# Attention sums shared anew between transfers, VectorE and GpSimd in a transformer block

## The reference

```python
h = _layernorm(x, axis=-1) * (1 + ca) + sa
x = x + ga * _L0_attn_ref(h, ...)      # 32 query heads, 8 key/value heads, head size 32
h = _layernorm(x, axis=-1) * (1 + cb) + sb
x = x + gb * _L0_ffn_ref(h, ...)       # top-2 of 4 experts, each a rank 16 product
```

```python
attn = jnp.einsum('bqhfd,bkhd->bhfqk', qg, k) * scale
att = jax.nn.softmax(attn, axis=-1)
a = jnp.einsum('bhfqk,bkhd->bqhfd', att, v)
```

## Time and profile before

| | |
|---|---|
| median of three runs | 2799.31 us |
| profiled execution | 2796.36 us |
| its span, first to last instruction | 2794.5 us |
| mean granted TensorE clock | 0.996 |
| TensorE busy (matmul) | 2750.2 us |
| VectorE busy | 2178.0 us |
| GpSimd busy | 1906.9 us |
| ScalarE busy | 1529.6 us |

### The profile page before, as it was taken

One profiled execution on the slowest core, in us unless ns is written; L12 is line 12 of the kernel. 1 busy time (PEld: TensorE's weight loads), 2 busy tenths in 40 slices (PEclk: granted clock), 3 DMA queues, 4 the chain that ended last, 5 costly groups with the idle time before them and its releaser, 6 DMA issues.

```text
span 2794.5 us, 49051 instructions
## 1 busy us (share of the span) xinstructions
PE 2750.2 (98%) x14654; PEld 1696.9 (61%) x14654; DVE 2178.0 (78%) x2809; ACT 1529.6 (55%) x3023; POOL 1906.9 (68%) x710
## 2 busy tenths in 40 slices
PE   7999999999999999999999999999999998999998
PEld 4788888884444444444444444444444447888887
DVE  4433334348999999999999999999999958676667
ACT  3211111116777776767777777767776763455454
POOL 2433333317999999999999999999999986111110
PEclk9999999999999999999999999999999999999999
DMA  7544443434444434344344344443444443323332
GB/s 267 182 144 137 147 137 135 135 114 133 92 88 99 91 87 100 85 87 100 85 92 95 85 98 89 91 98 84 96 93 87 99 132 102 114 96 108 113 100 81
DMA packets 167644, 307.05 MB, mean 110 GB/s; under 512 B 50000, under 2 KB 91408, under 8 KB 159504
## 3 DMA queue, kind: packets, MB, share of 16 engines
q1 hardware_dynamic: 158496, 240.05, 29.5%
q0 software_dynamic: 9072, 66.06, 11.6%
HBM read 159.12 MB, written 79.82 MB: 86 GB/s over the span
## 4 chain that ended last, share of the span: by engine, by line
PE 71%; POOL 3%; DVE 2%; issue 1%; ACT 0%; POOLq 0%; DVEq 0%; ACTq 0%
PE back_ps L1354 20%; PE back_ps L1368 17%; PE s_ps L1328 16%; PE s_ps L1944 12%; POOL p_sum L1129 3%; PE back_ps L1993 2%; PE back_ps L1385 2%; PE back_ps L2012 1%; PE back_ps L1965 1%; DVE mx L1243 0%; PE back_ps L1343 0%; ACT h_t L1725 0%; DVE xn L1799 0%; DVE two_sum L1258 0%; PE back_ps L2019 0%
## 5 line engine op out<-in xcount | busy, mean ns | idle before, releaser
L1223 ACT ACTIVATE p_t<-back_ps 128x512 f32<-128x512 f32 x2048 | 1114.6, 596 | 426.6 <-PE back_ps L1354 388.2
L1243 DVE TENSOR_REDUCE mx<-s_ps 128x1 f32<-128x1024 f32 x1002 | 1172.0, 1208 | 81.9 <-PE s_ps L1328 73.9
L1129 POOL TENSOR_TENSOR p_sum<-p_sum,p_t 128x2048 f32<-128x2048 f32 x254 | 1166.9, 4594 | 22.0 <-ACT p_t L1223 5.7
L1354 PE MATMUL back_ps<-q_st,k_st 98*128 98x512 f32 x2048 | 806.2, 434 | 4.2 <-POOL ones L1098 2.4
L1354 PEld LDWEIGHTS back_ps<-q_st,k_st 98*128 98x128 f32 x2048 | 343.9, 187 | 582.2 <-ACT p_t L1223 483.7
L1328 PE MATMUL s_ps<-k_st,q_st 96*128 96x512 f32 x2004 | 634.3, 397 | 0.7 <-DVE mx L1243 0.4
L1368 PE MATMUL back_ps<-p_t,v_sb 128*32 128x512 f32 x4096 | 546.4, 605 | 0.0
L1328 PEld LDWEIGHTS s_ps<-k_st,q_st 96*128 96x128 f32 x2004 | 379.3, 189 | 77.7 <-DVE mx L1243 8.8
L1258 DVE TENSOR_REDUCE two_sum<-p_t 128x512 f32<-128x1024 f32 x256 | 317.5, 1242 | 8.7 <-DMA p_sum<-two_sum 8.7
L574 POOL TENSOR_TENSOR o_lo<-side,o_hi 128x512 fp32r<-128x512 f32 x80 | 104.3, 1304 | 320.8 <-ACT o_hi L544 320.7
L1129 POOL TENSOR_TENSOR p_sum<-p_t 128x2048 f32<-128x2048 f32 x64 | 313.0, 4891 | 9.3 <-ACT p_t L1223 9.3
(11 more groups left out here) (186 smaller groups left out, 2917.9 us busy)
## 6 DMA issues: line engine op xcount, KB each, us to landing
p_sum<-two_sum POOLq DMA_DIRECT2D x63, 1024.0 KB, 6.9
q_st<-q_hi_d SPq DMA_DIRECT2D x128, 256.0 KB, 4.4
stage<-w_mod SPq DMA_DIRECT2D x48, 512.0 KB, 6.4
q_hi_d<-o_hi SPq DMA_DIRECT2D x64, 256.0 KB, 2.0
q_lo_d<-o_lo SPq DMA_DIRECT2D x64, 256.0 KB, 2.1
q_st<-q_lo_d SPq DMA_DIRECT2D x64, 256.0 KB, 4.1
att_d<-a_sb SPq DMA_DIRECT2D x128, 128.0 KB, 2.3
a_f<-att_d SPq DMA_DIRECT2D x32, 512.0 KB, 4.7
```

The lines of the kernel that those rows point to most:

```text
L1129: nc.gpsimd.tensor_tensor(total, before, p_t[:, kt, :, :], ALU.add).then_inc(sum_done, 1)
L1223: nc.scalar.activation(p_t[:, s, c, :], st_ps[:, c % 2, :], ACT.Exp, scale=SCALE)\
L1243: nc.vector.tensor_reduce(mx[:, slot % 2, e:e + 1], s_ps[:, e % 2, :], AX_X, ALU.max)\
L1354: nc.tensor.matmul(st_ps[:, c % 2, :], k_st[:, slot // 2, s * P:(s + 1) * P], q_st[:, slot, jj, h * QW:(h + 1) * QW], start=True, stop=True)\
```

## The change

Block by block, per pair:

- Blocks 6 and 7: a transfer issued by GpSimd (`merge`) adds block 6 to block 7 inside `p_t`, once TensorE has multiplied both. A second one (`join`) adds block 7 to `p_sum`. `two_sum` no longer goes through a transfer.
- Blocks 2 and 3: VectorE adds tiles 0 and 1 (`HALF`) of both into `two_sum`, in steps 4 and 5. GpSimd adds tiles 2 and 3 of each block into `p_sum` with two adds of 128x1024, and in the next pair adds `two_sum` to the first half of `p_sum` (`add_half`, 128x1024).
- Blocks 0+1, 4 and 5: GpSimd, whole. The division moves behind the half adds, ahead of block 4.
- GpSimd's order in a pair: `merge` and `add_half` of the pair before, blocks 0+1, `join` of the pair before, half adds, division, blocks 4 and 5.
- ScalarE's waits follow: block 6 waits for `merge`, block 7 for `join`, blocks 2 and 3 for both GpSimd's and VectorE's share.
- In the last pair VectorE adds all four tiles of 2+3, two in each of steps 4 and 5, and GpSimd adds 0+1, 4 and 5. SyncE's waits ahead of `bo` and `up_w` change places between `sum_done` and `two_done`.

```diff
-    ADDED = (0, 1, 2, 5, 6, 7)
-    SUMS = len(ADDED) - 1
+    SUMS = 6
+    USED_AT = {0: 1, 1: 1, 2: 2, 3: 3, 4: 4, 5: 5}
     LATE = (6, 7)
-    TWO = 3
-    TWO_STEPS = (5, 6, 7)
+    TWO = 2
+    HALF = REP // 2
+    TWO_STEPS = (4, 5)
...
-                sp.wait_ge(sum_done, pair * SUMS + 2)
+                sp.wait_ge(two_done, pair * HALF + REP)
                 sp.wait_ge(num_done, pair * STEPS + 3)
...
-                sp.wait_ge(two_done, NPAIR * REP)
+                sp.wait_ge(sum_done, pair * SUMS + 2)
                 sp.wait_ge(num_done, pair * STEPS + 5)
...
+        def merge(pair):
+            pool.wait_ge(num_done, pair * STEPS + STEPS)
+            pool.sem_inc(waited_pool, 1)
+            nc.gpsimd.dma_start(p_t[:, LATE[1], :, :].rearrange("p c q -> p (c q)"),
+                                p_t[:, LATE[0], :, :].rearrange("p c q -> p (c q)"), accum_op=ALU.add)\
+              .then_inc(merged, 16)
+
         def join(pair, par):
+            pool.wait_ge(merged, pair * 16 + 16)
             pool.wait_ge(sum_done, pair * SUMS + SUMS)
-            pool.wait_ge(two_done, pair * REP + REP)
             pool.sem_inc(waited_pool, 1)
             nc.gpsimd.dma_start(p_sum[:, par, :, :].rearrange("p c q -> p (c q)"),
-                                two_sum[:, :, :].rearrange("p c q -> p (c q)"), accum_op=ALU.add)\
+                                p_t[:, LATE[1], :, :].rearrange("p c q -> p (c q)"), accum_op=ALU.add)\
               .then_inc(joined, 16)
+
+        def add_half(pair, par):
+            half = p_sum[:, par, 0:HALF, :]
+            pool.wait_ge(two_done, pair * HALF + HALF)
+            pool.wait_ge(sum_done, pair * SUMS + 5)
+            nc.gpsimd.tensor_tensor(half, half, two_sum[:, 0:HALF, :], ALU.add).then_inc(sum_done, 1)
 
         def do(pair, slot, it):
             if not below(pair, 1):
-                join(pair - 1, (slot - 1) % 2)
+                merge(pair - 1)
+                add_half(pair - 1, (slot - 1) % 2)
...
+            nc.gpsimd.tensor_tensor(total, p_t[:, 0, :, :], p_t[:, 1, :, :], ALU.add).then_inc(sum_done, 1)
+            if not below(pair, 1):
+                join(pair - 1, (slot - 1) % 2)
+            made = 1
+            if not is_int(pair, NPAIR - 1):
+                for kt in (TWO, TWO + 1):
+                    pool.wait_ge(exp_done, pair * TILES + (kt + 1) * REP)
+                    pool.wait_ge(sum_done, pair * SUMS + made)
+                    nc.gpsimd.tensor_tensor(total[:, HALF:REP, :], total[:, HALF:REP, :], p_t[:, kt, HALF:REP, :], ALU.add)\
+                      .then_inc(sum_done, 1)
+                    made += 1
+            if not below(pair, 2):
+                divide(pair - 2, slot % 2)
+            for kt in (4, 5):
+                pool.wait_ge(exp_done, pair * TILES + (kt + 1) * REP)
+                pool.wait_ge(sum_done, pair * SUMS + made)
+                nc.gpsimd.tensor_tensor(total, total, p_t[:, kt, :, :], ALU.add).then_inc(sum_done, 1)
+                made += 1
...
+                    if s in USED_AT:
+                        act.wait_ge(sum_done, (pair - 1) * SUMS + USED_AT[s])
+                    if s in (TWO, TWO + 1):
+                        act.wait_ge(two_done, (pair - 1) * HALF + HALF)
+                    if s == LATE[0]:
+                        act.wait_ge(merged, (pair - 1) * 16 + 16)
+                    if s == LATE[1]:
+                        act.wait_ge(joined, (pair - 1) * 16 + 16)
...
             if c == 0 and not below(pair, 1):
-                dve.wait_ge(joined, pair * 16)
+                dve.wait_ge(sum_done, pair * SUMS)
...
-                if s == 0 and not below(pair, 1):
-                    add_two(pair - 1, REP - 1)
                 if s in TWO_STEPS:
                     add_two(pair, TWO_STEPS.index(s))
+                    if is_int(pair, NPAIR - 1):
+                        add_two(pair, HALF + TWO_STEPS.index(s))
...
-                pe.wait_ge(sum_done, pair * SUMS + SUMS - len(LATE))
+                pe.wait_ge(sum_done, pair * SUMS + 3)
...
-            pe.wait_ge(two_done, pair * REP + REP)
+            pe.wait_ge(two_done, pair * HALF + REP)
```

More of the change, by code:

```diff
@@ L853, in attend @@
     NS = HEADS * NKT
-    ADDED = (0, 1, 2, 5, 6, 7)
-    SUMS = len(ADDED) - 1
+    SUMS = 6
+    USED_AT = {0: 1, 1: 1, 2: 2, 3: 3, 4: 4, 5: 5}
     LATE = (6, 7)
-    TWO = 3
-    TWO_STEPS = (5, 6, 7)
+    TWO = 2
+    HALF = REP // 2
+    TWO_STEPS = (4, 5)
     SUM_STEP = 7
     DIVIDE_STEPS = (1, 2, 3)
-    DIVIDE_AFTER = 2
     TURN_STEP = 5
@@ L880, in attend @@
     assert PIECES == NPAIR // 2
-    assert KT == NKT and NS == 16 and sorted(ADDED + (TWO, TWO + 1)) == list(range(NKT))
+    assert KT == NKT and NS == 16 and LATE == (NKT - 2, NKT - 1)
     START_PLAN = [(1, e) for e in range(AHEAD - NS, NS)] + [(2, e) for e in range(NS // 2)]
@@ L948, in attend @@
     two_done = sem("two_done")
+    merged = sem("merged")
     joined = sem("joined")
     waited_pool = sem("waited_pool")
-    two_used = sem("two_used")
+    late_used = sem("late_used")
     num_taken = sem("num_taken")
@@ new lines, in do @@
+                add_half(pair - 1, (slot - 1) % 2)
+            total = p_sum[:, slot % 2, :, :]
+            pool.wait_ge(exp_done, pair * TILES + 2 * REP)
+            if not below(pair, 2):
+                pool.wait_ge(sum_used, pair - 1)
+            nc.gpsimd.tensor_tensor(total, p_t[:, 0, :, :], p_t[:, 1, :, :], ALU.add).then_inc(sum_done, 1)
+            if not below(pair, 1):
+                join(pair - 1, (slot - 1) % 2)
+            made = 1
[6 more added lines that the diff above has]
+                    made += 1
@@ L1265, in divide @@
                 if is_int(pair, NPAIR - 1):
-                    dve.wait_ge(two_used, 1)
+                    dve.wait_ge(late_used, 1)
                 nc.vector.transpose(den_t[:, :, :].rearrange("p c r -> p (c r)"), den_ps[:, :])\
@@ L1310, in vector @@
         pairs(dve, do)
-        add_two(NPAIR - 1, REP - 1)
         for pair in (NPAIR - 2, NPAIR - 1):
@@ L1398, in add_two @@
                                             start=False, stop=kt == LATE[-1])
-            done.then_inc(two_used, 1)
+            done.then_inc(late_used, 1)
         def after(pair, slot, s):
```

## The result

The changed kernel takes 2807.09 us (median of 8 runs, 2805.44 to 2808.47) beside 2799.28 us (8 runs, 2797.41 to 2801.08) of the kernel before: a ratio of 1.0029, 95% interval [1.0020, 1.0038]. It is slower, and above the whole range forecast. The code shown ahead of this is the old one; in the new kernel the score products for maxima are L1359, those for exponentials L1385, the numerator L1399, the denominator L1416, VectorE's maxima L1273, its adds L1288 and its subtraction of a weights' piece L1312. On GpSimd the transfers are L1110 and L1119, the adds L1140, L1156 and, with half the columns, L1129 and L1148, the division L1166.

A forecast was written before the change was run, and what follows sets the result against it. TensorE was taken to bound the kernel at 25.93 us a pair, GpSimd pacing later pairs; 3.5 us gained in attention and 2.2 lost at the hand-over gave -1.3, so 2798.0 us, range 2791.5 to 2806.

The forecast's parts named there:

- the one on VectorE: Steady attention pairs: VectorE loses two of four adds of 1.24 us a pair, which was to buy nothing.
- GpSimd's new pair: GpSimd's work per attention pair: 24.7 us against TensorE's 25.93, about 1.2 us of slack, so it stops pacing anything.
- rival C: GpSimd's half adds cost 2.83 us each, so it needs 26.1 us a pair: 2808 us in total, chance 0.07.
- The two transfers: GpSimd's transfers per pair: first lands at 10 us on the pair's clock, second at 18.1 to 19.4, cost zero.
- B: Rival: the second transfer lands after ScalarE's block 7 exponentials want it, at 21.5 of each pair; 2816.6 us, chance 0.08.
- (a): Later attention pairs: GpSimd's division ends 2.6 us earlier, SyncE's maxima transfer is issued ahead of need, 1.4 us gained.
- (b): Pair 0: VectorE, behind with 18 maxima, has two adds less, so three lengthened steps recover, 1.0 us gained.
- (c): Last pairs: one period of 26.25 us (0.32 over) and waits of 0.44 and 0.30 for the maxima's transfer go, 1.06 gained.
- The hand-over: Attention to last stage: VectorE's later split delays SyncE's x loads and the LoRA weights' landing, 2.2 us lost.

## Why the prediction was wrong

**The step that failed** is the one on VectorE: "In the steady pairs that buys nothing: its idle time is not on the path." I compared amounts: two adds of four less, so more idle time. I never placed the remaining two on the clock of a pair, though I did so for GpSimd. Four kernels give one line. The rows show how far the maxima ahead of m_lo start before (-) or behind (+) TensorE's numerator product, and the interval that begins with that product, in us:

```
adds in 5 and 6 (and the kernel before)  -0.71 (-0.72)   3.10
adds in 4 and 5, piece in step 3         -0.28           3.25
changed kernel (4 and 5, piece in 4)     -0.11           3.44
before, two adds in step 5               +0.44           3.96
```

Past the first row every 0.1 us later costs TensorE 0.1 us: 0.44 plus the offset gives 0.16, 0.33 and 0.88 over 3.10, where the intervals are 0.15, 0.34 and 0.86 over. The 0.44 is fitted to these rows, each from one pair, but all pairs bear them out: the medians of 27 pairs are -0.30 and 3.23, -0.11 and 3.44, +0.46 and 3.99, and the changed kernel's pairs without a piece, at -0.39 and 3.15, lie on the same line. Before the change VectorE was not early by much (0.28 us of room in this place) and nothing in the busy shares shows it. The cost in the changed kernel: 26.27 against 25.905 with adds in 5 and 6 is 0.36 in 30 pairs, 11 us; the other pairs give at most 0.02 each. Less some 2 us that the pace of GpSimd gave back over 60 pairs, that is the 9.7 measured. None of my rivals held it: they priced transfers, GpSimd and the hand-over, and VectorE appeared only as the one that is relieved.

**GpSimd's new pair**: right. 1.47 and 0.85 us of idle time in the pair shown, and no wait of TensorE for the maxima's transfer. A half add took 2.39, and 2.68 directly behind an issue, against 2.35 and 2.65 that I took and 2.83 at which rival C starts; the full ones 4.59.

**The two transfers**: right. The first lands after 8.4 at the median and 10.1 at most, where I had 10 on the clock (8 after its issue), the second after 6.9. B fell with that. That the old transfer took "6.9 every time" is not what its row says: its longest took 8.2.

**(a)** came in size: the kernels with adds in 5 and 6 keep 25.905 and 25.94 where the kernel before goes to 25.98. Its mechanism was only half right: the run with the maxima ahead of the store shows a second way, through VectorE's add that waits for the late transfer. **(b)** came as forecast: three intervals of pair 0, 3.42, 3.40 and 3.46 long before, are 3.10 each now. Of that 1.0 us the first pair with a piece takes 0.4 back. The 1.8 us to the first sum hold more, but that lies in the first step of attention: it took 5.9 us in this execution of the kernel before and 4.2 in the kernel before with the division first, whose code is the same there. **(c)** came in two of its three parts: 0.9 at the end for 0.74 forecast. The period of 26.25 stays 26.25, as it is one of the pairs with a piece; with adds in 5 and 6 it is 25.84.

**The hand-over**: a size near by with a wrong mechanism. Forecast was 2.2 us for the weights, measured 1.3. I had it come through the split: 3.02 us long, 7 us later, and x loads 2.2 us later. The split took 1.22 and the loads left 0.5 later; with the split back in its old place the loads of x leave 3.3 us earlier and the weights are not earlier. What the kernels with the second transfer have in common is a longer landing of the weights: 11.0 to 12.5 us for their later load, against 9.2 to 9.7 in the four with one transfer. Their scaling starts 5.5 to 6.4 us behind the last denominator product, against 4.56, 4.50 and 5.39 in the kernels with one transfer and the last pair as it was. I take the queue for the cause: the 1 MB transfer starts 17.7 us ahead of that product, 18.8 before, with SyncE's loads close behind. From its issue to the landing of the weights' later load the transfer engines are 0.93 busy before and 0.94 after (windows 2283.10 to 2306.40 and 2291.21 to 2314.75), and this stretch takes 23.1 to 24.0 us in all eleven kernels, whether the transfer starts 22.0, 18.8, 18.0 or 17.7 us ahead of the product. So the queue was full, as the prediction had it, but what the landing moves with is that transfer, 1.1 of the 1.3 us, and not the loads of x. No run moved that transfer alone, so this is argued and not shown. Another 0.8 us of the 9.1 lies in the last stage and stays open.

**What was left of the forecast without the failed step** shows in the kernel with adds in 5 and 6: 3.3 us less than the kernel before, where 1.3 less was forecast.

## What to carry to other kernels

Room on a double-buffered pair of engines is a matter of place, not of sum: before calling an engine's idle time cover, put its instructions on the clock of one period and look at how far ahead of its user each result is. Extra instructions belong in the steps with the longest period or ahead of an idle stretch, and two of them in neighbouring short steps count together, with any piece that comes only in every second period. Where a rate limit is removed at one wait, look for the second wait by which the same late engine reaches the same user.

## What the runs showed of the hardware beside that

VectorE's subtraction of two tiles in SBUF (128x1024) took 1.22 us with GpSimd idle (2294.39, above) and 4.80 in the kernel with adds in steps 5 and 6 (2277.10, above). GpSimd there:

```profile
2276.21 4.61 POOL L1140 TENSOR_TENSOR p_sum<-p_t 128x2048 f32<-128x2048 f32 x1 [0.47 <-ACT p_t L1253]
```

Its add ends at 2280.82, and the subtraction 1.08 us later, at 2281.90. The 3.02 us of the kernel before come out the same way: GpSimd's adds end there at 2282.49, and the subtraction 1.09 us later. The eleven traces have 18 such subtractions beside an add of GpSimd, 2.1 to 6.0 us long, and each ends 1.08 or 1.09 us behind the end of that add; the four without one took 1.21 or 1.22. So VectorE waited for the end of GpSimd's add and then worked at its own speed. GpSimd pays as well, if its next add is issued meanwhile. In the kernel before, the first tile's subtraction ran until 2262.74, and the add beside its end took 5.44 us instead of 4.59:

```profile
2261.79 5.44 POOL L1129 TENSOR_TENSOR p_sum<-p_sum,p_t 128x2048 f32<-128x2048 f32 x1
```

The Trainium skill (SBUF — State Buffer, "SBUF: two separate sides") states this as a lock on a shared pair of ports, taken by whichever starts first, for VectorE with two inputs in SBUF against a GpSimd instruction that reads SBUF; these rows agree. So the 3.02 us held a wait of 1.8 us, and to carry them to another place, as the prediction did, was unfounded. The adds that VectorE makes as a reduction took 1.22 to 1.28 us in the kernel before, though GpSimd was at work beside 255 of the 256.
